# Attention and feed-forward on one core: small denominator transfers ahead of the installs, the first batch standardised on VectorE, and one score-maximum unit between two projections

## What is computed

```python
x = x + attention(layernorm(x))        # 16 heads of 64, causal, masked scores are 1e-10 and not -inf
x = x + ffn(layernorm(x))              # 3 blocks of two 256x256 layers

# attention, per head
scores = keys . queries / 8; scores = where(q < k, 1e-10, scores)
out = softmax(scores) . values . W_output + Bias_output
# ffn weights, per layer: 4-bit codes with a scale per 16 columns, and a rank-32 addition
w = (q / 7.5 - 1) * repeat(scale, 16) + lora_b . lora_a
```

## Time and profile before

| | |
|---|---|
| median of 3 runs | 2349.63 us (2340.82 to 2351.74) |
| the profiled execution | 2349.61 us, its span 2346.8 us |
| PE busy | 2233.1 us, 95% |
| DVE, POOL, ACT busy | 1319.5 (56%), 1368.0 (58%), 918.7 us (39%) |
| DMA queue | 259.35 MB, 41.5% of 16 engines' span |
| the first score matmul of item 0 starts | 109.91 us |
| the attention part ends, the feed-forward part's first transfer is issued | about 1976 us, 1980.93 us |

### The profile page before, as it was taken

How to read it: one execution, slowest core, us unless ns; L and a number is a source line. 1 busy time by engine, 2 the same in 40 slices (tenths; PEclk the granted TensorE clock), 3 DMA queues, 4 the chain that set the end, 5 groups by cost and what they waited for, 6 DMA issues and landing times. The chain is left out here.

```text
span 2346.8 us, 31194 instructions
## 1 busy us (share of the span) xinstructions
PE 2233.1 (95%) x10080; PEld 1135.8 (48%) x10080; DVE 1319.5 (56%) x3555; ACT 918.7 (39%) x1780; POOL 1368.0 (58%) x1231
## 2 busy tenths in 40 slices
PE   5799999999999999999999999999999998899987
PEld 2244444444444444444444444444444445777764
DVE  4755555555555556464646565656555572466664
ACT  3244444444444445444444444444444442110110
POOL 2067776777777777677777676767676731211110
PEclk9699999999999999999999999999999998999999
DMA  3643626362626273535353535353636323421100
GB/s 89 140 113 80 167 76 161 81 167 77 169 74 169 79 192 79 146 97 146 99 146 98 152 91 147 96 152 90 158 85 172 99 74 103 164 80 46 63 18 18
DMA packets 206272, 261.33 MB, mean 111 GB/s; under 512 B 74720, under 2 KB 91296, under 8 KB 206112
## 3 DMA queue, kind: packets, MB, share of 16 engines
q1 hardware_dynamic: 206112, 259.35, 41.5%
HBM read 169.87 MB, written 88.87 MB: 110 GB/s over the span
## 5 line engine op out<-in xcount | busy, mean ns | idle before, releaser
L720 POOL TENSOR_TENSOR acc<-acc,probs 128x512 f32<-128x512 f32 (+1 forms) x900 | 996.8, 1141 | 290.5 <-ACT probs L1082 290.1
L1082 ACT ACTIVATE probs<-ps_s 128x512 f32<-128x512 f32 (+1 forms) x1152 | 603.5, 576 | 735.6 <-PE ps_s L874 452.2
L1147 DVE TENSOR_REDUCE partial<-ps_bg 128x1 f32<-128x512 f32 x768 | 489.0, 683 | 204.5 <-PE ps_bg L811 203.6
L872 PE MATMUL ps_s<-qq,kk 128*128 128x512 f32 (+3 forms) x1280 | 580.5, 454 | 9.9 <-DMA qm<-maxima 6.4
L893 PE MATMUL ps_o<-probs,v 128*64 128x512 f32 (+3 forms) x2560 | 542.6, 544 | 2.1 <-DVE num L1171 2.1
L874 PE MATMUL ps_s<-qm,kl 128*128 128x512 f32 (+3 forms) x1280 | 469.6, 367 | 0.0
L759 PE MATMUL ps_bg<-home,w_in 128*128 128x512 f32 x768 | 372.5, 609 | 8.5 <-ACT home L1024 3.9
L872 PEld LDWEIGHTS ps_s<-qq,kk 128*128 128x128 f32 x1280 | 244.6, 191 | 205.4 <-issue 145.8
L811 PE MATMUL ps_bg<-k_bf,q_bf 64*128 64x512 bf16 (+3 forms) x1280 | 251.2, 362 | 29.7 <-DVE split L1129 22.8
L893 PEld LDWEIGHTS ps_o<-probs,v 128*64 128x64 f32 x2560 | 155.6, 136 | 232.6 <-issue 185.3
L874 PEld LDWEIGHTS ps_s<-qm,kl 128*128 128x128 f32 x1280 | 243.9, 191 | 37.4 <-issue 21.6
(11 more groups left out here) (113 smaller groups left out, 1902.9 us busy)
## 6 DMA issues: line engine op xcount, KB each, us to landing
high_and_low<-split SPq DMA_DIRECT2D x128, 512.0 KB, 5.9
qq<-high_and_low SPq DMA_DIRECT2D x64, 512.0 KB, 4.4
kk<-high_and_low SPq DMA_DIRECT2D x128, 256.0 KB, 5.2
qm<-high_and_low SPq DMA_DIRECT2D x64, 256.0 KB, 6.0
kl<-high_and_low SPq DMA_DIRECT2D x64, 256.0 KB, 6.4
e<-masked_weights SPq DMA_DIRECT2D x128, 128.0 KB, 3.0
scale<-inverse_sums SPq DMA_DIRECT2D x128, 128.0 KB, 2.9
heads_turned<-num SPq DMA_DIRECT2D x64, 256.0 KB, 3.1
```

Source lines behind the costliest of these rows:

```text
L720: g.tensor_tensor(acc[h][:, group % 2, q0:q0 + w], acc[h][:, group % 2, q0:q0 + w], probs[h][:, probs_slot(i, t), at:at + w], ALU.add).the ...
L872: pe.matmul(out, kk[:, h, kb * P:(kb + 1) * P], qq[:, h, q], start=True, stop=False, skip_group_check=True)
L1082: nc.scalar.activation(probs[h][:, probs_slot(i, t), CH * half:end], ps_s[:, k % SCORE_BANKS, 0:end - CH * half], ACT.Exp, scale=SCORE_SCA ...
L1147: e.reduce_max(to, of, AX.X).then_inc(max_read, 1)
```

## The change

It has four parts.

- SP's list for an item is put in another order. `take_den` of groups 1 and 0 now stands ahead of `install_chunk` of chunks 1 and 0, `put_inverse` of group 1 goes to the start of the next item, `keep_max` and `keep_masked` of chunk 3 go ahead of `put_inverse` of group 3, and the stores move a little. `install_chunk` of chunk 0 waits behind `put_inverse` and `spread_inverse` of group 0. DVE inverts later: groups 3, 2, 1, 0 at slots 74, 110, 123, 132 instead of 68, 106, 118, 128 (123 and 132 are slots 3 and 12 of the next item), and POOL normalises one or two tiles later.
- Batch 0 is standardised by DVE: POOL makes only `rstd`, and DVE does one operation for 256 columns, subtract and multiply, four for a chunk.
- The head's order has the units one at a time: one maximum unit after each projection from the fourth on, where the old list has two together after most of them. DVE's statistics and standardising stand in the list too. For the second batch, the statistics, `rstd`, the standardising and the turns of chunks 1 and 0 come later.
- The six `dequantise` (two operations each on 128x512) move from POOL to DVE: four at slots 105, 106, 113 and 114 of the last item, two after its last denominators.

```diff
-INVERT_SLOT = {3: 68, 2: 106, 1: 118, 0: SLOTS + 8}
+INVERT_SLOT = {3: 74, 2: 110, 1: SLOTS + 3, 0: SLOTS + 12}
-NORMAL_TILE = {3: 13, 1: 2, 0: 4}
+NORMAL_TILE = {3: 15, 1: 3, 0: 5}
-FIRST_ORDER = [("proj", 0), ("turn", 2), ("proj", 1), ("proj", 2), ("proj", 3), ("max", 0), ("max", 1), ("turn", 1),
-               ("proj", 4), ("max", 2), ("max", 3), ("proj", 5), ("proj", 6), ("max", 4), ("max", 5), ("turn", 0),
-               ("proj", 7), ("max", 6), ("max", 7), ("proj", 8), ("proj", 9), ("max", 8), ("max", 9),
-               ("proj", 10), ("max", 10), ("max", 11), ("proj", 11)] + [("max", n) for n in range(12, NMAX)]
+FIRST_ORDER = [("turn", 3), ("proj", 0), ("turn", 2), ("stats", 1), ("proj", 1), ("norm", 1), ("proj", 2), ("proj", 3),
+               ("stats", 0), ("max", 0), ("turn", 1), ("proj", 4), ("norm", 0), ("max", 1), ("proj", 5), ("max", 2),
+               ("proj", 6), ("max", 3), ("turn", 0), ("proj", 7), ("max", 4), ("proj", 8), ("max", 5), ("proj", 9),
+               ("max", 6), ("proj", 10), ("max", 7), ("proj", 11)] + [("max", n) for n in range(8, NMAX)]
-STATS_AT = {3: 50, 2: 56, 1: 66, 0: 78}
-RSTD_TILE = {3: 10, 2: 11, 1: 13, 0: 15}
-XN_AT = {3: 67, 2: 73, 1: 85, 0: 97}
-TURN_AT = {3: 76, 2: 82, 1: 94, 0: 106}
+STATS_AT = {3: 50, 2: 56, 1: 78, 0: 84}
+RSTD_TILE = {3: 10, 2: 11, 1: 14, 0: 15}
+XN_AT = {3: 67, 2: 73, 1: 93, 0: 99}
+TURN_AT = {3: 76, 2: 82, 1: 102, 0: 108}
-CODES_TILE = [3, 4, 5, 6, 9, 10]
+CODES_AT = [105, 106, 113, 114]
...
                     if i:
+                        put_inverse(i - 1, 1)
                         spread_inverse(i - 1, 1)
-                        install_chunk(i, 0)
                         take_den(i - 1, 0)
                         install_max(i, 0)
                     if more:
                         keep_split(i + 1, 3)
-                    if i:
-                        put_inverse(i - 1, 0)
                     load_masked(i)
                     spread_masked(i, 3)
                     if i:
+                        put_inverse(i - 1, 0)
                         spread_inverse(i - 1, 0)
-                        store_heads(i - 1, 1)
+                        install_chunk(i, 0)
                     if more:
                         keep_split(i + 1, 2)
...
                     put_inverse(i, 2)
-                    masked_rows(i, 1)
                     spread_inverse(i, 2)
-                    if more:
-                        install_chunk(i + 1, 1)
                     take_den(i, 1)
                     masked_rows(i, 0)
                     if more:
+                        install_chunk(i + 1, 1)
                         keep_max(i + 1, 1)
                         keep_masked(i + 1, 1)
-                    put_inverse(i, 1)
-                    if more:
                         install_max(i + 1, 1)
                     store_heads(i, 2)
...
+                def standardise(c):
+
+                    n = ln_count(0, c)
+                    b = n % 2
+                    dve.wait_ge(rstd_done, START + n)
+                    for t in range(4):
+                        last = e.tensor_scalar(chunk_rows[c][:, t, :], chunk_rows[c][:, t, :], mv[:, b, t, 0:1],
+                                               rstd[:, b, t:t + 1], ALU.subtract, ALU.mult)
+                    last.then_inc(xn_done, 1)
...
+                        for l, at in enumerate(CODES_AT):
+                            if i == N - 1 and n == at:
+                                dequantise(l)
+                invert(N - 1, 1)
                 sum_denominators(N - 1, 0)
+                for l in range(len(CODES_AT), n_layers):
+                    dequantise(l)
                 invert(N - 1, 0)
```

More of the change, by code:

```diff
@@ L158, in background @@
     for kind, n in FIRST_ORDER:
-        if kind != "turn":
+        if kind in ("proj", "max"):
             order.append((kind, 0, n))
         if kind == "max":
-            order += [(kind, 0, c) for (kind, c), at in zip(FIN_FIRST, FIRST_FIN_AT) if at == n]
+            order += [(fin, 0, c) for (fin, c), at in zip(FIN_FIRST, FIRST_FIN_AT) if at == n]
     order += [(kind, 0, c) for (kind, c), at in zip(FIN_FIRST, FIRST_FIN_AT) if at == NMAX]
@@ L559, in _ @@
                     take_den(i, 3)
+                    if more:
+                        keep_max(i + 1, 3)
+                        keep_masked(i + 1, 3)
                     put_inverse(i, 3)
@@ L594, in _ @@
                         keep_masked(i + 1, 0)
+                put_inverse(N - 1, 1)
                 spread_inverse(N - 1, 1)
@@ L612, in invert_root @@
                     pool.wait_ge(var_done, START + n)
+                    g.tensor_tensor(rstd[:, n % 2], var_eps[:, n % 2], minus_half[:, :], ALU.pow).then_inc(rstd_done, 1)
+                    if batch == 0:
+                        return
                     g.tensor_scalar(minus_mean[:, n % 2], mv[:, n % 2, :, 0], -1.0, None, ALU.mult).then_inc(mean_done, 1)
-                    g.tensor_tensor(rstd[:, n % 2], var_eps[:, n % 2], minus_half[:, :], ALU.pow).then_inc(rstd_done, 1)
-                    pool.wait_ge(mean_done, START + n)
+                    pool.wait_ge(mean_done, START + n - 4)
                     pool.wait_ge(rstd_done, START + n)
@@ L728, in _ @@
                 normalise(N - 2, 0)
-                for l in range(4):
-                    dequantise(l)
                 masked_part(N - 1, 2)
-                for l in range(4, n_layers):
-                    dequantise(l)
                 normalise(N - 1, 3)
@@ L928, in _ @@
                         turn_x(0, n)
+                        continue
+                    if what != "max":
                         continue
@@ L1001, in masked_weight @@
                                          scale=-1.0).then_inc(e_ready, 1)
-                def standardise(batch, c):
-                    for t in range(4):
-                        standardise_tile(batch, c, t)
                 def standardise_tile(batch, c, t):
@@ L1042, in take_weight @@
                     nc.scalar.copy(w_t[l], bank("weight", 0, l)).then_inc(wt_ready, 1)
-                standardise(0, 3)
-                standardise(0, 2)
-                take_x(0, 3)
-                act.wait_ge(w_loaded, START + 144)
-                standardise(0, 1)
-                high(0, 0)
-                take_x(0, 2)
-                for u in (1, 2, 3):
-                    high(0, u)
-                standardise(0, 0)
-                take_x(0, 1)
-                for u in (4, 5, 6):
-                    high(0, u)
-                take_x(0, 0)
-                for u in range(7, NPROJ):
-                    high(0, u)
+                for what, n in FIRST_ORDER:
+                    if what == "turn":
+                        take_x(0, n)
+                        if n == 3:
+                            act.wait_ge(w_loaded, START + 144)
+                    elif what == "proj":
+                        high(0, n)
                 act.wait_ge(consts, START + 1)
@@ L1186, in invert, with dequantise @@
                     e.reciprocal(inverse[:, :, :], den_sq[:, :, :]).then_inc(inverse_ready, 1)
+                def dequantise(l):
+                    if l == 0:
+                        dve.wait_ge(ffn_w_loaded, START + 16 * 6)
+                    e.tensor_scalar(w_unit[l], w_q[l], 1.0 / 7.5, -1.0, ALU.mult, ALU.add).then_inc(w_units, 1)
+                    dve.wait_ge(w_units, START + l + 1)
+                    by_group = w_unit[l].rearrange("p h (k e) -> p (h k) e", e=16)
+                    e.tensor_tensor(by_group, by_group,
+                                    sc_in[:, halves * l:halves * l + halves, :].rearrange("p h k -> p (h k)").unsqueeze(2)
+                                    .to_broadcast([P, halves * D // 16, 16]), ALU.mult).then_inc(w_dequant, 1)
                 def add_last(t):
@@ L1249, in chunk_stats @@
                     e.tensor_scalar(var_eps[:, b], mv[:, b, :, 1], LN_EPS, None, ALU.add).then_inc(var_done, 1)
-                row_stats(0, 3)
-                row_stats(0, 2)
+                def standardise(c):
[6 more added lines that the diff above has]
+                    last.then_inc(xn_done, 1)
+                for c in (3, 2):
+                    row_stats(0, c)
+                    standardise(c)
                 dve.wait_ge(w_loaded, START + 144)
-                row_stats(0, 1)
                 for what, n in FIRST_ORDER:
-                    if what == "proj":
+                    if what == "stats":
+                        row_stats(0, n)
+                    elif what == "norm":
+                        standardise(n)
+                    elif what == "proj":
                         low(0, n)
-                        if n == 0:
-                            row_stats(0, 0)
                     elif what == "max":
```

29 lines of the change are left out of this document (9 added, 20 removed).

## The result

| | before | after |
|---|---|---|
| median of 20 runs each, in turn | 2346.86 us | 2332.49 us |
| ratio, 95% interval | | 0.9947 (0.9935 to 0.9960) |
| span of the profiled execution | 2346.8 us | 2331.6 us |

The change gains 14.4 us by the medians (12.4 us by the ratio) where 32.4 us were forecast; the time lies just above the range's upper end of 2332 us. The forecast started from 2349.6 us, which is 2.7 us above the median of these 20 runs, so the time misses by 15.3 us and the gain by 18.0 us.

What follows compares the result with a forecast made beforehand. PE was taken to bound the items, DVE and the DMA queue the head's later part. Terms 16.7 + 3.5 + 4.7 + 8.5 - 1.0 = 32.4 us, from 2349.6 to 2317.2 us; range 2305 to 2326, widened to 2303 to 2332 us.

Steps and rivals of the forecast that it cites:

- The head: Part 1, up to the first score matmul: 16.7 us gained, bounds 4 to 20 us.
- the chains: End of the head: DVE's work done at 90.7 us, SP's list giving the first score at 91.5 us; gain 18.4 us.
- the half-clock stretch: Middle of the head: one slow PE stretch allowed for at half of 3.4 us, lowering the gain from 18.4 to 16.7 us.
- Part 2: SP's order in the items: late den_sq waits go, 3.5 us gained, between 0 and 5.8 us.
- it is covered, by 1 to 2 us: Split write of chunk 2 in the items: lands at about 500 us, before ACT's copy needs its buffer at 501.40 us.
- the last rival: Whole kernel: moved units only shift waits, row of maxima late anyway, pairs bound by PE; 2339 us, chance 0.06.
- The rival of the late split write: Items: chunk 2's late write makes ACT and PE wait in 14 items, 14 us per microsecond; 2366 us at 3.5 us; chance 0.06.
- Part 3: Item with the second batch: later slots remove DVE's wait and the half-clock stretch; 4.7 us gained, between 0 and 5.3 us.
- Part 4: Last item: PE's waits of 3.4 and 2.1 us and some missing clock go; 8.5 us gained, between 5.5 and 10.9 us.
- 3.0 us of missing clock: Last item: share of the window's 5.4 us of missing clock counted as gain, as mostly the aftermath of PE's waits.
- The end: After the last item: group 2's later inverse delays the last store; 1.0 us lost, between 0 and 5 us.
- The codes: Last item: twelve dequantise operations on DVE, some 0.7 us each, lie in its idle time and cost nothing.

Runs made afterwards that it cites:

- E8: Changed kernel with group 1's row of maxima before install chunk 1, the last item's install chunk 0 before take_den of group 0, group 2's last inverse at slot 106; 2314.1 us.
- E9: Kernel before with only the change's head and second-batch slots; SyncE's order, inverse slots and codes as before; 2324.6 us.
- E7: Changed kernel with the second batch's statistics, standardising and turning slots put back as before; 2335.8 us, ratio 0.9972.
- E1: Kernel before with only the change's head (order of units, batch 0 standardised on DVE); 2327.0 us.
- E5: Changed kernel with, in the last item only, install chunk 0 ahead of take_den of group 0 and group 0's reciprocal 24 slots later; 2323.3 us.
- E11: Kernel of E8 with the write of split 2 also ahead of install chunk 0 in every item but the last; 2313.8 us.
- E6: Changed kernel with the codes dequantised on GpSimd again, as before; 2336.1 us, ratio 0.9956.
- E3: Changed kernel with group 1's row of maxima and masked weights issued ahead of install chunk 1 in every item; 2329.4 us.

## Why the prediction was right and wrong

**The head was right in size and in its steps.** First turn 16.57 us (16.6 forecast), first projection 19.70 us (19.8), next weights 54.67 us (54.9), first score 92.55 us (91.5 by the chains, 93.2 with the half-clock stretch counted). VectorE's work in the middle was 23.1 us (23.5). The half-clock stretch that I counted, 1.7 us, did not come: the middle is at 1.00. Here the row decides for the rule that the prediction weighed: the Trainium skill (TensorE: Matmul & The Clock Gate, What's actually happening) has half speed as the default that activity releases, and the denser middle kept the full clock. What I took for the clock went to the end of the head instead, where 37.9 us (54.67 to 92.55 us) stand for the 36.6 us taken over from before. That the sum came within 0.7 us is luck in so far as these two errors cancel, and kernels with this head scatter by more than that.

**Part 2, SyncE's order, failed in its cover.** The gain is there: TensorE's waits at L759 are gone and so are VectorE's, and in the traces E8's items, with the new waits removed, are 7.2 us shorter than E9's, where 3.5 us were forecast. The failed step is "it is covered, by 1 to 2 us". Counted from the item's first score (458.9 us in the trace of before, 439.6 us in that of after), I had put the issue of split 2 at +34.1 us and its landing at +41.1 us; it was issued at +36.2 us and landed at +44.7 us. SyncE was 2.1 us later than by my reading of its list. It stood at the row of group 1's maxima (issued at 449.80 us behind install chunk 1, read back at 455.35 us), a wait that the reading left out: in the pair of before the row was read back 1.4 us after its issue, since SyncE had by then stood for `den_sq` behind the same install. That the row of maxima is late anyway was the last rival, at 0.06. And the write took 8.5 us behind 1.5 MB of installs where I had allowed 7; the median of 5.9 us is one transfer's, while a write has two, and the pair of before had taken 6.9 us with no install in flight ahead of it. So 3.6 us were missing on a cover of 1 to 2 us. In six items ScalarE stood, 13.3 us together, and four of these waits reached TensorE, 5.3 us together, one with a half-clock stretch behind it. The rival of the late split write was this mechanism at a smaller size: it took every item as hit by the same amount, while the items scatter around the limit.

**Part 3, the second batch, was right:** 4.7 us forecast, 5.1 us in the item (126.9 to 121.8), 3.6 us by undoing it (E7), 4.4 us between the traces of E1 and E9.

**Part 4, the last item, had the wrong sign.** Forecast 8.5 us of gain, measured 3.4 us of loss: 11.9 of the 17.2 us by which the sum was off in the two traces (32.4 - 15.2), its largest error. The failed step is the assumption, taken over from part 2, that the moved transfers find the last item as they find the others. It has no projections, so its slots follow each other faster, while SyncE's list takes as long as ever. I worked out slot 30 at the pace of an ordinary item and never asked for it in the last. E5 shows the term: with the install back in its place the last item takes 83.9 us, 6.8 us less than before, close to the 82 us forecast. Most of the 8.5 us are there to be had (6.3 to 8.0 us in E5, E8 and E11), but not with install chunk 0 behind `spread_inverse`. Even so the term was read from a single execution: its 3.0 us of missing clock were at least in part chance, since E1 has nearly the same waits at the full clock and an item of 86.1 us, against which the three kernels gain only 1.7 to 3.4 us.

**The end was right in its place, not in its size.** That the later slot of group 2's inverse would hold up what follows was foreseen, priced at 1.0 us up to 5 us through the last store. The last store was issued at 1958.22 us and ScalarE's last copy ended at 1959.66 us; that copy came 20.1 us behind the last weighted-sum matmul in place of 18.6 us, since TensorE had waited 1.4 us for the last `den_rows`. The store landed 2.0 us after its issue, 0.6 us behind the copy. The term that was left out is that wait and the clock behind it, up to 11 us. No row of before shows it, for there was none.

**The codes** cost nothing that can be told (E6): VectorE takes 0.41 and 0.69 us for the two operations where I had estimated 0.7 us each.

**The range and a rival.** The bounds of the five terms add up to gains of 4.5 to 42.0 us, that is 2307.6 to 2345.1 us. The range of 2305 to 2326 us that the prediction draws from them does not come out of them, and the measured time lies inside the wider one. The last rival's own terms (parts 3 and 4 and the end) give 12.2 us and 2337.4 us, not 10 us and 2339 us.

## What to carry to other kernels

A transfer that is moved back in a queue must be checked against its user in every kind of item, above all in the last, where work is missing and slots are short while the queue's list keeps its length. When a transfer that the queue waits for is taken from behind a large one, ask what it waits for next: here the stall passed from `den_sq` to a row of 4 KB, and with the row first, in the last item, to the transfer after it. Waits on an engine off the critical path are worth only what they hand on, here 4.8 us of 188.1 us in E9's items, and it is the bounding engine's own waits, new ones too, that must be counted. A stage whose code is not changed shows how far single profiles differ; a term read from one profile can hold that much chance.

## What the runs showed of the hardware

A short wait of TensorE can be followed by a loss of several times its length through the granted clock. In the turnover a wait of 1.3 to 1.5 us was followed by nothing, by 6.8 us at 0.50, or by 0.50 to the end of the turnover, in seven kernels with the same wait; none of the seven kernels without the wait has a turnover over 29.1 us. E3's stretch stayed at 0.50 for 19.0 us although TensorE counted as busy all the time, so by that row being busy did not by itself release the half speed. Waits of 5.2 us in the last item of E1 were followed by no drop of the clock.

A small transfer lands behind the large ones issued just before it: the two 512 KB transfers of a split write took 8.5 us behind an install, against 6.9 us for the pair of before in the earlier trace rows, and the row of maxima, 4 KB, 5.6 us behind an install (449.80 to 455.35 us, until SyncE could go on), against 1.4 us in before with the install already landed (469.17 to 470.57 us). The Trainium skill (DMA: Bandwidth & Descriptors, Queues, rings and completion order) says that on each DMA engine descriptors are consumed in ring order, though a later one may finish its write before an earlier one; the delays agree with the first.

VectorE's additions take nearly twice as long beside GpSimd's operations. In the last item of before, 14 of them took 15.76 us while GpSimd worked (masked part, normalising, dequantising), 1.13 us each; four while it stood idle took 2.50 us, 0.63 us each.

```profile
1897.84 15.76 DVE L1206 TENSOR_TENSOR acc<-acc,probs 128x512 f32<-128x512 f32 x14
...
1916.28 2.50 DVE L1206 TENSOR_TENSOR acc<-acc,probs 128x512 f32<-128x512 f32 x4
```
